# Expert rows stored in slot order and fetched back per token instead of scatter-added; half of the shared tiles moved to the end

## The chip, the cores and the metric

One core of a Trainium2 chip runs the whole program. The metric is the device time of one launch in microseconds (us), lower is better. The engines are named as in the profile: PE (TensorE matmul), PEld (its weight loads), DVE (VectorE), ACT (ScalarE), POOL (GpSimd) and SP (SyncE, which here only issues DMAs). POOL's DMAs go through the software queue q0, those of SP and ACT through hardware queues.

## The reference, cut to what matters

A token embedding, a causal attention of 16 heads, and a mixture of experts over 2048 tokens with 512 channels. The change lies in the last part:

```python
logits = xt @ Wr.T + bias                      # xt: layer-normed rows, 2048 x 512
topk_val, topk_idx = top_k(softmax(logits), 2) # 16 experts
w = topk_val / (sum(topk_val) + EPS)
g, u = einsum('th,ehi->tei', xt, Wg), einsum('th,ehi->tei', xt, Wu)   # i = 256
y = einsum('tei,eih->teh', silu(g) * u, Wd)
routed = einsum('tke,tk,teh->th', one_hot(topk_idx), w, y)
shared = silu(xt @ sWg) * (xt @ sWu) @ sWd
return (routed + shared) + h                   # h: the residual
```

## The kernel before

The tokens are 16 tiles (NT) of 128 rows. After the attention (up to about 640 us) a loop makes the output projection, the second layer norm and the router logits of every tile. `acc[:, c, :]` holds the residual rows of tile c in SBUF; the normed rows go to `xn2_dram`, and turned into `xnT`.

Then come 16 shared tiles (`for n in range(SHARED)` in `moe_pe`, `moe_dve`, `moe_act`): gate and up as split matmuls (three matmuls of 512 columns for each k, L1180), the silu on ACT, the product on DVE (`gate`, L1108), two transposes (L1262), high and low parts (`turn_high` on ACT, `turn_low` on DVE, L1114), the down matmuls (L1273), and `shared_add` (L1119), which adds them to acc. POOL splits the rows of tile c into high and low parts (`split_rows`). SP's `store` writes each finished acc tile to `out`.

Between these tiles DVE and PE make the routing plan. `weights` normalises the two probabilities and makes the one-hots of the choices. `ranks` (PE, after shared tile 3) counts. `places` and `choice_places` give each of the 2 x 2048 choices a slot: slots are grouped by expert and padded to tiles of 128, so there are at most 47 tiles (TILES = 2 * 16 + 15). `slot_onehots` makes three small one-hots for each of 32 pairs of choice and tile, and `slots` (PE, L1243) multiplies them into bank 1: for every slot its token number and its weight. `slot_tokens` turns these into `slot_tok`, `slot_w` and `slot_out` (spare slots get a row behind the output's end). Only then may POOL gather rows.

The 47 expert tiles are loops over pairs of tiles. For tile n PE's `routed` runs two k-steps of gate and up (L1252), the transposes of tile n-1's gated rows, two more k-steps, the transposes of the next tile's gathered rows (`turn_rows`, L1295), and tile n-1's down matmuls (`down_of`, L1331). SP loads expert e+4 into a ring of four (`w_gu`, in the space of `attnT`, and `w_dn`) when expert e's last tile is done, and waits for it to land before it looks at the next one. ACT's `y_scale` (L936) multiplies a tile's result by `slot_w` into one of two `y_sb` buffers. POOL's order is: `gather` of one tile (copy of the row numbers, L829, then an indirect DMA, L832), then `add` of an earlier one (L843, L846), an indirect DMA that adds y_sb to rows of `out` in DRAM. Each add waits for the one before to have landed (`s_yadd`), because two slots can name one token:

```python
pool.wait_ge(s_yc, 2 * m + (s + 1))
if not first:
    pool.wait_ge(s_yadd, 16 * (2 * m + s))
```

The first add also waits until all 16 tiles of acc are stored. The program ends when the last add has landed.

## Time and profile before

| | before |
|---|---|
| median of 3 runs | 1129.62 us (1126.68 to 1134.97) |
| profiled execution, span | 1135.9 us |
| PE busy | 1009.3 us, 89% |
| DVE busy | 560.7 us, 49% |
| ACT busy | 498.4 us, 44% |
| POOL busy | 328.1 us, 29% |
| chain that ended last, largest line | DMA out<-y_sb,out_no 15% |
| DMA, share of 16 engines: hardware queue q1, software queue q0 | 24.9%, 12.1% |

The profile is of one execution; its span is 6.3 us over the median of the other runs. Busy shares are means over stages with different limits: a change is read from the stage it touches. A wait is charged to what released it last. "Issue" is time in which an engine waited for nothing that the profile shows.

### The profile page before, as it was taken

What the parts mean: (1) busy time and instruction counts of PE and PEld (TensorE: products, weight loads), DVE (VectorE), ACT (ScalarE), POOL (GpSimd) and SP (SyncE); (2) the same over time, 40 slices, a digit from 0 to 9 for tenths busy, and PEclk for the clock granted to TensorE, in tenths of its full rate; (3) what the DMA queues carried; (4) which work ended last, traced back from release to release, by engine and by line L of the source; (5) the groups of instructions that cost most, each with busy time, mean ns of one, the idle gap of its engine ahead of it and who ended that gap; (6) DMA issues with size and microseconds to landing.
All of it is one profiled execution on the core that took longest, in us unless ns stands there. A gap on an engine that the chain in (4) does not pass through costs nothing.

```text
span 1135.9 us, 22815 instructions
## 1 busy us (share of the span) xinstructions
PE 1009.3 (89%) x6879; PEld 641.0 (56%) x6880; DVE 560.7 (49%) x1422; ACT 498.4 (44%) x1195; POOL 328.1 (29%) x444
## 2 busy tenths in 40 slices
PE   3766789999989999899998899899898998899994
PEld 1323547677665857567685687778543443344441
DVE  8986336565644756365666677578311111111110
ACT  4802167676756767476768522211121222122221
POOL 4068311110101010010202046333144543444442
PEclk9969989999989999899999999899899999999997
DMA  0023624150523324042335111611396448744442
GB/s 11 29 50 106 171 56 109 38 127 16 117 65 75 76 51 100 31 103 48 76 79 184 57 66 56 260 47 49 97 290 186 78 89 238 231 86 86 81 89 40
DMA packets 40395, 109.11 MB, mean 96 GB/s; under 512 B 9252, under 2 KB 9252, under 8 KB 37986
## 3 DMA queue, kind: packets, MB, share of 16 engines
q1 hardware_dynamic: 27970, 81.89, 24.9%
q0 software_dynamic: 12320, 25.90, 12.1%
q8 instruction: 55, 0.90, 0.3%
q14 instruction: 50, 0.41, 0.1%
HBM read 53.03 MB, written 25.17 MB: 69 GB/s over the span
## 4 chain that ended last, share of the span: by engine, by line
PE 56%; DMA 16%; issue 10%; DVE 9%; POOL 4%; ACT 2%; POOLq 1%; ACTq 0%; DVEq 0%
DMA out<-y_sb,out_no 15%; PE psum L511 10%; PE psum L477 7%; PE psum L524 6%; PE psum L498 6%; PE psum L482 5%; PE psum L1252 4%; PE psum L1196 4%; PE psum L1180 3%; PE psum L1331 2%; PE psum L1273 1%; PE psum L500 1%; PE psum L527 1%; DVE nmax L634 1%; DVE oh_lo L1488 1%
## 5 line engine op out<-in xcount | busy, mean ns | idle before, releaser
L634 DVE TENSOR_REDUCE nmax<-psum 128x1 f32<-128x128 f32 (+7 forms) x256 | 192.2, 753 | 80.2 <-PE psum L500 69.3
L593 ACT ACTIVATE probs<-psum,nmax 128x128 f32<-128x128 f32 (+7 forms) x256 | 190.4, 744 | 52.1 <-DVE nmax L634 46.9
L1252 PE MATMUL psum<-attnT,x_T 128*128 x376 | 183.2, 610 | 10.8 <-issue 9.4
L498 PE MATMUL psum<-k_stack,q_stack 128*128 128x512 f32 (+2 forms) x384 | 157.8, 465 | 24.1 <-issue 15.6
L511 PE MATMUL psum<-ident,probs 128*128 128x128 f32 x1152 | 175.7, 279 | 3.4 <-DVE probsT L580 1.5
L1153 DVE COPY x_T<-psum 128x512 f32<-128x512 f32 x47 | 32.5, 691 | 253.0 <-PE psum L1295 253.0
L578 ACT COPY probsT<-psum 128x512 f32<-128x512 f32 (+3 forms) x256 | 128.9, 503 | 57.0 <-PE psum L511 44.7
L477 PE MATMUL psum<-xnT,w_unit 128*128 128x512 f32 x256 | 132.4, 607 | 0.2 <-ACT full L452 0.2
L511 PEld LDWEIGHTS psum<-ident,probs 128*128 128x128 f32 x1152 | 125.2, 143 | 8.9 <-DVE probsT L580 3.8
L424 POOL CAST part_hi<-full 128x512 fp32r<-128x512 f32 x32 | 19.6, 612 | 378.7 <-ACT full L452 270.8
L1252 PEld LDWEIGHTS psum<-attnT,x_T 128*128 128x128 f32 x376 | 65.8, 193 | 90.0 <-issue 89.7
L498 PEld LDWEIGHTS psum<-k_stack,q_stack 128*128 128x128 f32 x384 | 69.4, 203 | 66.7 <-issue 33.5
L1331 PE MATMUL psum<-w_dn,gated_T 128*128 x188 | 88.6, 594 | 1.0 <-ACT gated_T L905 1.0
L846 POOL DMA_INDIRECT out<-y_sb,out_no x47 | 75.4, 1604 | 44.4 <-POOL out_no L843 44.4
L524 PE MATMUL psum<-probsT,v_unit 128*32 128x128 f32 x2304 | 78.8, 282 | 0.8 <-ACT probsT L578 0.8
L936 ACT ACTIVATE y_sb<-psum,slot_w 128x512 f32<-128x512 f32 x47 | 32.3, 687 | 105.8 <-PE psum L1331 101.9
L524 PEld LDWEIGHTS psum<-probsT,v_unit 128*32 128x32 f32 x2304 | 61.2, 113 | 28.7 <-ACT probsT L578 19.4
L648 DVE TENSOR_TENSOR attnT<-psum,z_rows 128x128 f32 (+1 forms) x64 | 18.6, 291 | 117.3 <-ACT z_rows L600 117.3
L482 PE MATMUL psum<-w_unit,xnT 128*128 128x128 f32 x512 | 66.7, 275 | 0.3 <-DVE full L456 0.3
L580 DVE COPY probsT<-psum 128x128 f32<-128x128 f32 (+3 forms) x128 | 61.6, 481 | 2.7 <-PE psum L511 2.6
L832 POOL DMA_INDIRECT x_rows<-xn_scratch,rows_no x47 | 50.0, 1064 | 42.2 <-POOL rows_no L829 36.1
L482 PEld LDWEIGHTS psum<-w_unit,xnT 128*128 128x128 f32 x512 | 61.8, 192 | 0.5 <-issue 0.5
(223 smaller groups left out, 1507.8 us busy)
## 6 DMA issues: line engine op xcount, KB each, us to landing
attnT<-in_wgu SPq DMA_DIRECT2D x16, 1024.0 KB, 5.1
q_stack<-part_hi SPq DMA_DIRECT2D x64, 128.0 KB, 2.4
q_stack<-part_lo SPq DMA_DIRECT2D x64, 128.0 KB, 2.4
k_stack<-part_hi SPq DMA_DIRECT2D x64, 128.0 KB, 2.4
k_stack<-part_lo SPq DMA_DIRECT2D x64, 128.0 KB, 2.5
w_dn<-in_wd SPq DMA_DIRECT2D x16, 512.0 KB, 6.0
out<-acc SPq DMA_DIRECT2D x17, 256.0 KB, 2.1
h_scratch<-hot_vec SPq DMA_DIRECT2D x16, 256.0 KB
```

The costliest lines, as they stand in the source:

```text
L477: mm = pe.matmul(bank(7), w_unit[:, k, side * P:(side + 1) * P], xnT[:, k, t0:t0 + 512], start=(k == 0), stop=(k == KC - 1), skip_group_ch ...
L482: mm = pe.matmul(bank(7)[:, k * P:(k + 1) * P], xnT[:, c, t0:t0 + P], w_unit[:, c, 2 * P:3 * P], start=(c == 0), stop=(c == KC - 1))
L498: mm = pe.matmul(dst[:, c0:c1], qs, k_stack[b][:, h, c0:c1], start=True, stop=not own)
L511: mm = pe.transpose(bank(4 + m % 2)[:, (j - 4 * k) * P:(j - 4 * k + 1) * P], probs[n % PSLOTS][:, j * P:(j + 1) * P], ident[:, :])
L524: pe.matmul(bank(6)[32 * h:32 * h + 32, 0:P], v_unit[b][:, j, 32 * h:32 * h + 32], probsT[i % 2][:, h, j * P:(j + 1) * P], start=(j == 0), ...
L578: eng.copy(dst, src).then_inc(s_Ca, 1)
L580: eng.tensor_copy(dst, src).then_inc(s_Cd, 1)
L593: act.activation(probs[n % PSLOTS][:, 0:(i + 1) * P], bank(2 * (n % 2), 2)[:, 0:(i + 1) * P], ACT.Exp, bias=nmax[:, n % 4:n % 4 + 1], scal ...
L634: dve.tensor_reduce(nmax[:, n % 4:n % 4 + 1], bank(2 * (n % 2), 2)[:, 0:(i + 1) * P], AX.X, ALU.min).then_inc(s_M, 1)
L846: pool.indirect_dma_start(out=out, out_offset=bass.IndirectOffsetOnAxis(ap=out_no[s][:, :], axis=0), in_=y_sb[:, s, :], in_offset=None, bo ...
L1252: mm = pe.matmul(bank(2 + p), lhs(k), rhs(k), start=(k == 0), stop=(k == KC - 1), skip_group_check=True)
L1331: mm = pe.matmul(bank(6 + p), gated_T[:, p, k * P:(k + 1) * P], w_dn[:, bass.ds(half, 1), k, :].rearrange("p o n -> p (o n)"), start=(k == 0),
```

## The change

Two things are done.

**Scatter to store and fetch.** ACT copies a tile's result unscaled into `y_sb` (`y_copy`) and issues a plain DMA of the 128 rows to a new DRAM tensor `y_dram`, in slot order (`y_store`, two tiles behind). POOL has only gathers in the expert loop. When all 47 stores have landed, POOL fetches for each token tile the two rows of each token (32 indirect DMAs, indices `pos_i`) into a ring of eight tiles, `y_back`, in the space of `attnT`. DVE's `add_choices` adds them, scaled by `w_top`, to acc with two `scalar_tensor_tensor` each. SP stores acc tiles only after that.

**Shared tiles moved.** Only 8 shared tiles (NS) run ahead of the experts, the other 8 behind them. The plan, which was spread over shared tiles 2 to 14, is now made in tiles 2 to 7, with up to 11 one-hot pairs in a tile (it was 5 triples) and a ring of 12. `slot_w`, `slot_pad` and `slot_out` are no longer made, and the weights are computed after the last expert tile. In the tail the splitting of rows (tiles 10 to 15) is on ACT and DVE; POOL splits 8 and 9 early in the expert loop.

The core of the diff:

```diff
-SLOT_RING = 6
-SLOT0 = 6
+SLOT_RING = 12
+SLOT0 = 5
+SLOT_STEP = 11
+NS = 8
+COMB0 = 3
+Y_RING = 8
...
+        def tail_no(c):
+
+            return NS + TILES + (c - NS)
+
+        def pass_of(c):
+
+            return c if c < NS else tail_no(c)
```

SP:

```diff
-            for c in range(NT):
-                store(c)
-
-            sp.dma_start(out[T:T + P, :], acc[:, 0, :]).then_inc(s_pad, 16)
...
-            sp.wait_ge(s_yadd, 16 * TILES)
+            for c in range(NS):
+                sp.wait_ge(s_comb, c + 1)
+                store(c)
```

POOL:

```diff
+            for c in (NS, NS + 1):
+                split_rows(c)
             with pool.Fori(2, TILES // 2) as m:
                 gather(m, 0, False)
-                add(m - 2, 1, False)
                 gather(m, 1, False)
-                add(m - 1, 0, False)
             gather(TILES // 2, 0, False)
-            for j in range(TILES - 4, TILES):
-                add(j // 2, j % 2, False)
+
+            for s in range(2):
+                pool.wait_ge(s_yst[s], 16 * ((TILES + 1 - s) // 2))
+            for c in range(NT):
+                if c >= Y_RING:
+                    pool.wait_ge(s_comb, c - Y_RING + 1)
+                passed(pool)
+                for k in range(TOPK):
+                    pool.indirect_dma_start(
+                        out=y_back[:, c % Y_RING, k, :], out_offset=None, in_=y_dram,
+                        in_offset=bass.IndirectOffsetOnAxis(ap=pos_i[:, k, c:c + 1], axis=0),
+                        bounds_check=TILES * P - 1, oob_is_err=False).then_inc(s_coldg[c % Y_RING], 16)
```

ACT:

```diff
+            def y_copy(n, q, first):
+
+                act.wait_ge(s_y, n + 1)
                 if not first:
...
+                    act.wait_ge(s_yst[q], stored(n, q))
+                act.copy(y_sb[:, q, :], bank(6 + q)).then_inc(s_yc, 1)
...
+            def y_store(j, q):
+
+                act.wait_ge(s_yc, j + 1)
+                rows = slice(j * P, j * P + P) if isinstance(j, int) else bass.ds(j * P, P)
+                act.dma_start(y_dram[rows, :], y_sb[:, q, :]).then_inc(s_yst[q], 16)
...
+            for c in range(NS, NT):
+                n = tail_no(c)
+                if c == NS:
+                    turn_copy(n - 1, 0)
+                else:
+                    turn_high(n - 1)
+                silu(n, n % 2)
+                if c == NS:
+                    y_store(LAST - 1, 1)
+                    y_copy(n - 1, 0, False)
+                    y_store(LAST, 0)
+                if c + 2 < NT:
+                    split_high(c + 2)
+            turn_high(tail_no(NT - 1))
```

DVE:

```diff
+            def add_choices(c):
+
+                r = c % Y_RING
+                dve.wait_ge(s_coldg[r], 16 + 16 * TOPK * (c // Y_RING + 1))
+                step(dve.scalar_tensor_tensor(out=acc[:, c, :], in0=y_back[:, r, 0, :], scalar=w_top[:, c, 0:1],
+                                              in1=acc[:, c, :], op0=ALU.mult, op1=ALU.add))
+                dve.scalar_tensor_tensor(out=acc[:, c, :], in0=y_back[:, r, 1, :], scalar=w_top[:, c, 1:2],
+                                         in1=acc[:, c, :], op0=ALU.mult, op1=ALU.add).then_inc(s_comb, 1)
+                dve.wait_ge(s_comb, c + 1)
...
+            for c in range(NS, NT):
+                if c > NS:
+                    turn_low(c - 1)
+                gate(tail_no(c), tail_no(c) % 2)
+                if c + 2 < NT:
+                    split_low(c + 2)
+                if c > NS + 1:
+                    shared_add(c - 2)
+                if c >= NS + COMB0:
+                    for t in range(2 * (c - NS - COMB0), 2 * (c - NS - COMB0) + 2):
+                        add_choices(t)
+            turn_low(NT - 1)
+            shared_add(NT - 2)
+            shared_add(NT - 1)
+            for t in range(2 * (NT - NS - COMB0), NT):
+                add_choices(t)
```

PE:

```diff
+            for c in range(NS, NT):
+                n = tail_no(c)
+                shared_gate_up(c, 0, 2)
+                turn_gated(n - 1, (n - 1) % 2)
+                shared_gate_up(c, 2, KC)
+                if c == NS:
+                    down_of(n - 1, 0, LAST, expert_half(LAST))
+                else:
+                    shared_down(c - 1)
```

In DVE's shared loop `choices` (the one-hots of the choices, without the weights) runs in tile 2, `places` in 3, `choice_places` in 4, one-hots 0 to 31 in 5, 6 and 7 (11, 11 and 10), `tile_experts` in 6. PE takes one-hots 0 to 10 behind shared tile 6's turn, 11 to 21 behind 7's and the last ten after the loop.

## Rows read from the trace of the kernel before

**Rows 1.** The chain that ended last, 780 to 1136: start, us, what

```profile
1002.55 4.86 DMA out<-y_sb,out_no
...
1008.82 4.69 DMA out<-y_sb,out_no
```

**Rows 2.** The timeline of PE, 800 to 900: start, us, engine, line, operation

```profile
821.62 1.88 PE L1252 MATMUL psum<-attnT,x_T 128*128 x4
...
825.28 0.60 PE L1295 MATMUL psum<-ident,x_rows 128*128 128x128 f32 x4
...
827.43 1.88 PE L1252 MATMUL psum<-attnT,x_T 128*128 x4
```

**Rows 3.** The timeline of PE, around 906, a pair's boundary

```profile
905.37 0.66 PE L1295 MATMUL psum<-ident,x_rows 128*128 128x128 f32 x4
...
908.13 1.98 PE L1252 MATMUL psum<-attnT,x_T 128*128 x4 [0.39 <-issue]
```

**Rows 4.** Busy time by stretch: us, each engine's busy us, granted clock, DMA share, GB/s

```profile
833.58:1111.96 278.38, 255.97 (x756) 114.81 (x757) 42.77 (x84) 60.58 (x126) 128.02 (x167) 1.00 0.59 138
...
724.00:728.00 4.00, 3.48 (x10) 2.76 (x11) 2.81 (x14) 0.58 (x2) 0.10 (x1) 0.57 1.02 423
```

**Rows 5.** The timeline of DVE, 738 to 800: the plan between the shared tiles

```profile
744.68 0.17 DVE L1046 COPY count_e<-psum 128x16 f32<-128x16 f32 x1
...
747.82 0.41 DVE L1114 TENSOR_TENSOR gs_lo<-psum,gs_hi 128x256 fp32r<-128x256 f32 x1
...
748.48 0.68 DVE L1119 TENSOR_TENSOR acc<-acc,psum 128x512 f32<-128x512 f32 x1
749.08 0.41 DVE L1063 TENSOR_TENSOR pos_all<-psum,base_e 128x256 f32<-128x256 f32 x1
...
752.10 0.20 DVE L1071 CAST pos_hlf<-pos_hl 128x64 f32<-128x64 int32 x1
...
754.32 0.83 DVE L1086 TENSOR_SCALAR slot_lo<-iota_f,pos_hlf 128x128 f32<-128x128 f32 x1
...
756.12 0.27 DVE L1086 TENSOR_SCALAR slot_lo<-iota_f,pos_hlf 128x128 f32<-128x128 f32 x1
...
756.74 0.27 DVE L1086 TENSOR_SCALAR slot_lo<-iota_f,pos_hlf 128x128 f32<-128x128 f32 x1
...
794.06 1.54 DVE L1075 TENSOR_TENSOR cmp_j<-tiles_to,iota_j 128x752 f32<-128x752 f32 x1
```

**Rows 6.** The timeline of POOL, 715 to 800 and on

```profile
753.76 1.30 POOL L802 TENSOR_TENSOR xs_lo<-xnT,xs_hi 128x512 fp32r<-128x512 f32 x1
...
800.19 0.18 POOL L829 COPY rows_no<-slot_tok 128x1 int32<-128x1 int32 x1 [5.39 <-DVE slot_out L1102]
```

**Rows 7.** The timeline of PE: shared tiles, then the first expert tile

```profile
740.05 0.48 PE L1180 MATMUL psum<-ws_hi,xs_hi 128*128 128x512 f32 x1
...
744.49 0.39 PE L1180 MATMUL psum<-ws_hi,xs_hi 128*128 128x512 f32 x1
...
805.43 0.63 PE L1295 MATMUL psum<-ident,x_rows 128*128 128x128 f32 x4 [2.17 <-DMA x_rows<-xn_scratch,rows_no]
...
807.22 3.77 PE L1252 MATMUL psum<-attnT,x_T 128*128 x4 [1.16 <-DVE x_T L1153]
```

**Rows 8.** The timeline of POOL, 70 to 140: indirect DMAs back to back

```profile
72.17 1.00 POOL L1413 DMA_INDIRECT hot_vec<-in_hot_emb,hot_row  x1 [0.30 <-issue]
73.47 0.99 POOL L1409 DMA_INDIRECT cold_lat<-in_cold_emb,cold_row  x1 [0.30 <-issue]
```

**Rows 9.** DMA issues of the whole run: count, KB each, median us to landing

```profile
w_dn<-in_wd SPq DMA_DIRECT2D x16, 512.0 KB, 6.0
out<-acc SPq DMA_DIRECT2D x17, 256.0 KB, 2.1
...
x_rows<-xn_scratch,rows_no POOLq DMA_INDIRECT x47, 3.8
```

**Rows 10.** The timeline, 1090 to 1136: the last instruction on POOL

```profile
1126.29 1.57 POOL L846 DMA_INDIRECT out<-y_sb,out_no  x1 [0.93 <-POOL out_no L843]
```

More of the change, by code:

```diff
@@ L284, in build @@
         s_on = sem("out_row_numbers_copied")
-        s_yadd = sem("y_added")
+        s_yst = [sem(f"y_stored{i}") for i in range(2)]
+        s_comb = sem("choices_added")
         s_pad = sem("spare_rows_stored")
@@ L328, in build @@
         s_hotg = [sem(f"hot_gathered{i}") for i in range(NT)]
-        s_coldg = [sem(f"cold_gathered{i}") for i in range(NT)]
+        s_coldg = [sem(f"cold_then_y_gathered{i}") for i in range(NT)]
         s_coldT = sem("cold_turned")
@@ L763, in moe_sp @@
                                          max_val=TILES)
-                    sp.wait_ge(s_y, done + SHARED)
+                    sp.wait_ge(s_y, done + NS)
                     load(WRING * m + s, s)
                     ready(m, s)
-            sp.wait_ge(s_yadd, 16 * TILES)
+            for c in range(NS):
+                sp.wait_ge(s_comb, c + 1)
+                store(c)
+            sp.dma_start(out[T:T + P, :], acc[:, 0, :]).then_inc(s_pad, 16)
+            for c in range(NS, NT):
+                sp.wait_ge(s_comb, c + 1)
+                store(c)
+            sp.wait_ge(s_out, 16 * NT)
+            sp.wait_ge(s_pad, 16)
         def moe_pool(pool):
@@ L815, in moe_pool @@
                     split_rows(c - NT + 3)
-            for c in range(2, NT):
+            for c in range(2, NS):
                 split_rows(c)
@@ L912, in turn_high @@
                 act.copy(gs_hi[:, n % 2, :], bank(4 + n % 2)[:, 0:FF]).then_inc(s_gshi, 1)
-            for n in range(SHARED):
+            for n in range(NS):
                 if n >= 1:
@@ L917, in moe_act, with routed @@
                 silu(n, n % 2)
-            def routed(m, s, first, added):
-                n = SHARED + 2 * m + s
+            def routed(m, s, before, first):
+                n = NS + 2 * m + s
                 q = 1 - s
-                if first:
+                if before < 1:
                     turn_high(n - 1)
@@ L941, in moe_act @@
-            routed(1, 0, False, None)
-            routed(1, 1, False, 16)
-            with act.Fori(2, TILES // 2) as m:
-                routed(m, 0, False, 16 * (2 * m - 2))
-                routed(m, 1, False, 16 * (2 * m - 1))
-            routed(TILES // 2, 0, False, 16 * (LAST - 2))
-            turn_copy(SHARED + LAST, 0)
-            y_scale(SHARED + LAST, 0, 16 * (LAST - 1))
+                if before >= 2:
+                    y_store(2 * m + (s - 2), s)
+                if before >= 1:
+                    y_copy(n - 1, q, first)
@@ L1275, in shared_down @@
                 mm.then_inc(s_y, 1)
-            for n in range(SHARED):
+            for n in range(NS):
                 if n:
@@ L1345, in moe_pe @@
             routed(TILES // 2, 0, True, None)
-            turn_gated(SHARED + LAST, 0)
-            down_of(SHARED + LAST, 0, LAST, expert_half(LAST))
+            for c in range(NS, NT):
+                n = tail_no(c)
[6 more added lines that the diff above has]
+                    shared_down(c - 1)
+            n = tail_no(NT - 1)
+            turn_gated(n, n % 2)
+            shared_down(NT - 1)
         @block.sync
```

145 lines of the change are left out of this document (69 added, 76 removed).

## Prediction

> **What bounds the kernel now.** I read the page's chain first, then the chain of 780 to 1136 alone, then the timelines of PE and POOL in that stretch, and last those of DVE and PE from 725 to 806. Up to shared tile 2 nothing is touched, so only three stretches count: the front (from there to the first expert tile), the expert loop, and what follows the last expert tile.
>
> In the expert loop the chain runs from scatter to scatter: each takes 4.7 to 4.9 us to land, and the next starts 6.27 us after it [rows 1]. The adds wait for each other, and POOL does the gathers between them, so POOL's round of 6.2 us also sets when rows arrive. PE alone would be quicker: an unrolled tile, with its rows there in time, takes 827.43 - 821.62 = 5.81 us [rows 2]. The 42 tiles from the fifth to the last took 278.4 us [rows 4], 6.63 each, or 13.26 a pair. At the boundary of a pair PE shows a gap that no engine is charged with, and the first gate matmul starts 2.76 us after the row transposes [rows 3] where 2.16 would do (the transposes' 0.43 and the down matmuls' 1.72, between the starts in rows 2). I take this as PE's queue, held at the wait for the gathered rows and not able to read ahead over the loop's branch and register loads. If so, the gap comes from a late gather too.
>
> **The front.** Anchors: PE starts shared tile 4 at 740.05 and the next at 744.49, 4.44 us a tile [rows 7], of which gate and up with its transposes are 3.0 and down 1.4 (12 and 6 matmuls of the 18). Without four small weight operations DVE lets PE reach tile 4 about 0.6 us sooner, and `places` now runs at once after `ranks`, at 739.5. From here DVE is the chain. `places` takes 747.82 - 744.68 = 3.14, `choice_places` 752.30 - 749.08 = 3.2; turn_low and gate start 0.33 apart and shared_add takes 0.60 [rows 5]. Added up, one-hot 0 starts at 749.2. A triple takes 756.74 - 756.12 = 0.62, so a pair 0.41 [rows 5]; the first still meets POOL's split, where such an operation took 0.83 and not 0.27 [rows 5, 6], 0.55 more. Eleven pairs end at 754.25. Only then comes turn_low(5), for which PE has waited 2.4 us. PE's down (1.4) frees the ring at 756.4; ten more pairs, 760.6; `tile_experts` 2.65 (1.54 and the two behind it), 763.3; turn_low(6), PE having waited 2.3 us; down, ring free at 765.4; nine pairs, 769.1; PE's last slot matmuls and two operations, 770.1. POOL starts at 770.2 where it started at 800.19 [rows 6], and the first transposes come 5.24 us later [rows 6, 7], at 775.5.
>
> To that I add PE's clock. Rows show it at 0.57 of full, its 1.2 GHz level for most of the stretch, from 724 to 728, behind a wait for the gate [rows 4], and the first expert tile's four matmuls took 3.77 us where four take 1.72 to 1.88, behind waits of 2.17 and 1.16 us [rows 2, 7]. The two new waits of 2.4 and 2.3 us are as long. A down and its slots at the low level cost 1.4 us more, once or twice, some of it under DVE's work: 1.5 in all (bounds 0 and 3.5). The first transposes start at 777.0 instead of 805.4: **28.4 us gained** (22 to 30). The low clock of the first expert tile is in both.
>
> **The expert loop.** The scatters (47 of about 4.8 us) leave; POOL has one gather per tile, about 2.1 us of work and 3.8 to land [rows 9], started when the buffer is free two tiles before it is needed, 11.6 us ahead. Rows are then never late. ACT copies as it did and gets a DMA issue per tile; ACT is 44% busy. A store lands in 2.1 us [rows 9], its buffer is wanted 5.8 us after the issue: covered; a store slower than that would hold y_copy, and down_of behind it. POOL's two `split_rows`, some 4 us, stand once ahead of tile 4's gather and use up a part of its 11.6. SP's weight loads keep their rule: expert e+4 is asked for two tiles ahead of its use, 11.6 us, and both its parts are in 6.5 us later (6.0 for w_dn, issued 0.5 behind [rows 9]) with the scatter beside them; where experts have one tile each, SP's wait for the landing lets the slack shrink by 0.7 a tile, and six such tiles don't end it. I take 11.75 us a pair (11.62 by rows 2, and a little for the branch): 21 pairs 246.8 us, **31.6 us gained**. Bounds: the scatter's pace of rows 1 stays, 12.54 a pair (263.3, gained 15.1); 11.62 (gained 34.4).
>
> **Behind the last expert tile**, counted from its first gate matmul (1111.96 before). PE finishes it in 5.81 less the transposes, 5.4. `weights`, 0.9 us of small operations, runs on an idle DVE behind the last expert tile's gate. Shared tile 8 takes 4.7, with the last expert's down ending at 10.1; y_copy 0.7 (L1119's 0.68 for the same block [rows 5]), issue 0.4, landing 2.1 [rows 9], a start of 0.3, and POOL fetches from 13.6 on. Indirect DMAs stood 1.30 us apart back to back [rows 8]; 32 of them: the last starts at 13.6 + 31 * 1.30 = 53.9 and lands at 57.7. The ring never holds them, for DVE is ahead of it. DVE starts to add in tile 11, when PE has done 5.4 + 4.7 + 2 * 4.44 + 3.0 = 22.1. Its round is then turn_low and gate 0.66, split_low 0.6, shared_add 0.6 and four adds. The trace has no scalar_tensor_tensor of 512 columns from SBUF; the nearest is L1119, 0.68 [rows 5]. With a semaphore between them 0.72 (bounds 0.6 and 1.1): a round is 4.74, more than PE's 4.44, and with the turn through PE and ACT 5.0 to 5.2. So PE is held to DVE's pace. SP's stores of acc, moved from the front to here, go out tile by tile beside the fetches and hold nothing but the last one. The last shared_add ends near 49.2. Six tiles of adds at 1.44 end at 57.8; but the last waits for the fetch, 57.7 + 1.44 = 59.1. Store 2.5, 61.6. From the last landing to the end of the span were 1135.9 - (1126.29 + 4.7) = 4.9 us [rows 1, 10]: 66.5 in all, against 23.9 before: **42.6 us lost** (38 to 55).
>
> **The sum.** 28.4 + 31.6 - 42.6 = 17.4 us gained, 1135.9 to 1118.5 in the profiled execution. That span is 6.3 over the median, so the same difference gives 1129.6 - 17.4 = 1112.2.
>
> **A rule against it.** In the tail POOL makes descriptors for 42 us while DVE reads two SBUF tensors at a time. In the row of 754.32 a DVE operation on SBUF ends at 755.15, just behind POOL's of 753.76 to 755.06 [rows 5, 6]: there one waited for the other to finish. The indirect DMAs of rows 8 kept 1.30 beside DVE work that read mostly PSUM. The Trainium skill's page SBUF — State Buffer (section SBUF: two separate sides) says that the pair of ports which VectorE and GpSimd share is locked for a whole instruction, by a VectorE operation in a two-port mode, or with two SBUF inputs against a GpSimd operation that reads SBUF. The trace agrees with it in that row; whether making descriptors counts as such an operation no row here shows. What it would do is the second rival below, priced from rows.
>
> **The rivals.**
> - The loop keeps its gap: PE's pause at a boundary is the loop's own and no late gather's, 2.76 - 2.16 = 0.60 us a pair [rows 3]. For it: it stands where no engine is named. Against it: the queue had been held at the rows' wait just before. 12.22 a pair, 256.6 us, 9.8 less: 1122; at the bound of 12.54 it is 1129.
> - The other side: in the tail each fetch and each add wait for each other. A fetch then comes every 1.30 + 0.69 = 1.99 us instead of 1.30; 31 * 0.69 = 21.4 more: 1134, slower than before. It decides from 1.30 + 17.4 / 31 = 1.86 us on.
> - The front gives less: DVE's plan loses more to ring waits and to PE's clock (for it: PE then stands over 2 us twice), and the first transposes start at 783, the bound above, 6 us less: 1118.
> - The better case: no clock loss (1.5), 11.62 a pair (2.8), and the tail at its bound of 38 (4.6): 1103.
>
> **How the numbers follow.** Forecast 0.58 (own range 1106 to 1118); better case 0.08; weaker front 0.09; loop with its gap 0.14; the lock 0.09, with the rest 0.02 for the lock together with the bound of 12.54 (1150). The range 1102 to 1128 leaves out the lock and the outer ends. One per cent, about what a measurement can tell from no change, is 1118.3 and 1140.9. Faster: 0.58 nearly whole, 0.08 and part of the front case, 0.67; slower by over 1% where the lock meets another loss, the 0.02 and a third of the 0.09, 0.05; same 0.28.
>
> **What would show it.** First row transposes 27 to 30 us sooner; PE waits for turn_low (L1114's successor) of over 2 us twice in the front; pairs of expert tiles at 11.6 to 11.9 us with no gap at the boundary and no wait for x_rows; 32 fetches 1.30 us apart; DVE adds of 0.7 us; PE's tail tiles near 5 us. Fetches over 1.8 us apart, pairs over 12.3, or a first transpose after 783 would each make it wrong.

## The result

The changed kernel took **1137.45 us** (median of 11 runs, 1135.32 to 1143.70) against 1129.73 us (11 runs, 1126.52 to 1137.31) for the kernel before: ratio **1.0069, 95% interval 1.0049 to 1.0090**. It is slower by 0.7%, which the interval tells from no change though it is less than the 1% that the prediction took for one, and the forecast of 1112 us with its range of 1102 to 1128 is wrong, in its sign too.

The same kernel was then measured five more times, on four chips. On three of them it was faster than the kernel before (0.9913 with 0.9882 to 0.9944; 0.9909 with 0.9879 to 0.9939; 0.9959 with 0.9936 to 0.9983; one single run each at 1128.15 against 1137.65), on the fourth it was slower again, by little (1.0023, 1.0001 to 1.0045). One of six executions of the changed kernel on chip 0 (1209.88 us) and one of 17 of the kernel before (3452.72 us) were slow; the ratios leave them out. The middle of this document is about what divides them.

### The profile of the changed kernel

The profiled execution spans 1139.1 us (the kernel before: 1135.9). First the page's busy times, then PE's timeline where the front ends.

```profile
PE 1008.7 (89%) x6879; PEld 653.7 (57%) x6880; DVE 577.4 (51%) x1424; ACT 497.0 (44%) x1201; POOL 262.9 (23%) x370
```

Columns: start us, us, engine, line, operation, tiles, count, and in brackets the idle time before and what ended it.

```profile
753.71 0.50 PE L1349 MATMUL psum<-ws_hi,gs_hi 128*128 128x512 f32 x1 [1.93 <-DVE gs_lo L1152]
...
777.34 1.09 PE L1372 MATMUL psum<-ident,x_rows 128*128 128x128 f32 x4 [5.68 <-DMA x_rows<-xn_scratch,rows_no]
...
779.43 3.37 PE L1324 MATMUL psum<-attnT,x_T 128*128 x4 [1.00 <-DVE x_T L1200]
```

The first row transposes stand at 777.34, where [rows 7] have 805.43. The loop, from the same view:

```profile
896.39 1.88 PE L1408 MATMUL psum<-w_dn,gated_T 128*128 x4
898.11 1.88 PE L1324 MATMUL psum<-attnT,x_T 128*128 x4
...
901.76 0.60 PE L1372 MATMUL psum<-ident,x_rows 128*128 128x128 f32 x4
902.20 1.88 PE L1408 MATMUL psum<-w_dn,gated_T 128*128 x4
903.92 1.88 PE L1324 MATMUL psum<-attnT,x_T 128*128 x4
...
931.41 2.78 PE L1324 MATMUL psum<-attnT,x_T 128*128 x4 [2.98 <-SPq L754]
...
946.70 1.98 PE L1324 MATMUL psum<-attnT,x_T 128*128 x4 [1.72 <-SPq L754]
```

Tiles start 5.81 us apart (898.11, 903.92), row transposes to next gate 2.16 with no gap: the boundary of [rows 3] is gone, and so is the chain of scatters of [rows 1]: gathers are the only indirect DMAs left in the loop. But PE stands still for weights (L754 is SP's report that they have landed), and the tile after the longer stop runs its matmuls slowly: 2.78 us for four instead of 1.88. From the fifth to the last expert tile the loop takes from 803.83 to 1057.19, 253.4 us against 278.4 in [rows 4].

Behind the last expert tile, first POOL, then ACT with PE's transposes that ACT waits for:

```profile
1071.02 1.00 POOL L875 DMA_INDIRECT attnT<-y_scratch,pos_i  x1 [24.74 <-DMA y_scratch<-y_sb]
1072.32 1.00 POOL L875 DMA_INDIRECT attnT<-y_scratch,pos_i  x1 [0.30 <-issue]
...
1107.67 1.00 POOL L875 DMA_INDIRECT attnT<-y_scratch,pos_i  x1 [0.30 <-issue]
1114.99 1.00 POOL L875 DMA_INDIRECT attnT<-y_scratch,pos_i  x1 [6.32 <-DVE acc L1166]
```

```profile
1087.89 0.38 PE L1334 MATMUL psum<-ident,gated 128*128 128x128 f32 x2
...
1096.25 0.79 PE L1349 MATMUL psum<-ws_hi,gs_hi 128*128 128x512 f32 x1 [6.58 <-issue]
...
1100.72 0.38 PE L1334 MATMUL psum<-ident,gated 128*128 128x128 f32 x2
...
1111.80 0.79 PE L1349 MATMUL psum<-ws_hi,gs_hi 128*128 128x512 f32 x1 [9.31 <-DVE gs_lo L1152]
```

```profile
1077.88 0.37 ACT L923 CAST gs_hi<-psum 128x256 fp32r<-128x256 f32 x1 [2.07 <-PE psum L1334]
...
1095.30 0.37 ACT L923 CAST gs_hi<-psum 128x256 fp32r<-128x256 f32 x1 [7.66 <-remote]
1098.14 0.38 ACT L910 ACTIVATE silu_g<-psum 128x256 f32<-128x256 f32 x1 [2.46 <-remote]
...
1110.85 0.37 ACT L923 CAST gs_hi<-psum 128x256 fp32r<-128x256 f32 x1 [11.82 <-remote]
```

This is where the time went. ACT's copy at 1110.85 needs the transposes that PE's record has at 1100.72 to 1101.10. "remote" is what the view says when a signal came whose sender had been done long before. Matching PE's signals in the trace with the recorded ends of the matmuls that send them gives this (us):

```
sent by              recorded end   arrived   late
shared down L1349       1080.63     1081.71    1.1
transposes L1334        1082.21     1083.85    1.6
gate and up L1253       1083.61     1086.72    3.1
shared down             1086.69     1090.28    3.6
transposes              1088.27     1095.28    7.0
gate and up             1089.67     1098.11    8.4
shared down             1099.18     1103.79    4.6
transposes              1101.10     1110.82    9.7
gate and up             1102.48     1110.90    8.4
```

Everywhere else in this trace PE's signals arrive 0.01 to 0.02 us behind the recorded end (two more, at 78.95 and 79.96, are 0.2 and 0.7 late); those of ACT and POOL are never late. The ends of matmuls are modelled in a profile, so one must ask whether the matmuls themselves were late. The last two lines speak against it: 1.38 us of gate and up matmuls lie between the recorded ends 1101.10 and 1102.48, and the two signals arrive 0.08 us apart (0.07 on chip 14, below). While PE waits, the granted clock falls: its mean over 1088 to 1100 is 0.72, so a part of it ran at the 1.2 GHz level. The tail, from the last expert tile's first gate matmul (1057.19) to the end, is 81.9 us; the forecast had 66.5, the kernel before 23.9.

The ledger: front 28.1 us gained, the four tiles behind it 1.7, loop 25.0, tail 58.0 lost; 3.2 lost in all, 1135.9 to 1139.1.

### The profile page after: what moved, and what is told of

Its sections match the earlier page's. It is cut to its first block, busy times and chain, and to the rows that moved or that the text cites. A ratio compares the mean times of both kernels' runs of the same rounds, so it can differ in the third digit from the quotient of the medians.

```text
span 1139.1 us, 22668 instructions
## 1 busy us (share of the span) xinstructions
PE 1008.7 (89%) x6879; PEld 653.7 (57%) x6880; DVE 577.4 (51%) x1424; ACT 497.0 (44%) x1201; POOL 262.9 (23%) x370
## 4 chain that ended last, share of the span: by engine, by line
PE 61%; issue 14%; DVE 9%; DMA 6%; POOL 3%; another core or an unknown queue 3%; ACT 2%; SPq 1%; ACTq 0%; DVEq 0%; POOLq 0%
PE psum L518 10%; PE psum L484 7%; PE psum L1324 7%; PE psum L531 6%; PE psum L505 6%; DMA w_dn<-in_wd 5%; PE psum L489 5%; PE psum L1269 4%; PE psum L1408 3%; PE psum L1253 3%; PE psum L1349 2%; PE psum L534 1%; PE psum L507 1%; POOL hot_vec L1500 1%
## 5 line engine op out<-in xcount | busy, mean ns | idle before, releaser
L1324 PE MATMUL psum<-attnT,x_T 128*128 x376 | 180.2, 602 | 7.6 <-SPq L754 4.7
L505 PE MATMUL psum<-k_stack,q_stack 128*128 128x512 f32 (+2 forms) x384 | 157.4, 464 | 23.8 <-issue 13.8
L1324 PEld LDWEIGHTS psum<-attnT,x_T 128*128 128x128 f32 x376 | 68.3, 193 | 76.9 <-issue 76.9
L949 ACT COPY y_sb<-psum 128x512 f32<-128x512 f32 x47 | 27.5, 585 | 84.2 <-PE psum L1408 54.6
L910 ACT ACTIVATE silu_g<-psum 128x256 f32<-128x256 f32 x63 | 24.2, 384 | 83.5 <-PE psum L1324 64.1
L507 PE MATMUL psum<-mask_bf,ident_bf 128*128 128x128 bf16 x256 | 59.7, 233 | 0.0
```

Of the source, the lines that this page charges most:

```text
L505: mm = pe.matmul(dst[:, c0:c1], qs, k_stack[b][:, h, c0:c1], start=True, stop=not own)
L507: mm = pe.matmul(dst[:, i * P:(i + 1) * P], ident_bf[:, :], mask_bf[:, :], start=False, stop=True)
L1324: mm = pe.matmul(bank(2 + p), lhs(k), rhs(k), start=(k == 0), stop=(k == KC - 1), skip_group_check=True)
```

## The experiments

Times are compared with the kernel before on the same chip. "Tail" is always from the first gate matmul of the 47th expert tile to the end of the span; line numbers shift by some lines from kernel to kernel.

### The unaltered kernel again: do the late signals belong to it?

> The changed kernel unaltered, looked at once more. In the one trace of it so far, nine of TensorE's signals between 1080 and 1103 us arrive 1.1 to 9.7 us after the recorded ends of their matmuls, and the tail takes 81.9 us from the first matmul of the 47th expert tile. If that belongs to the kernel (theory PAIR: it comes of VectorE's full-width adds together with GpSimd's fetches), the tail is again 75 to 88 us, with three or more such waits of ScalarE of over 2.5 us. If it was an accident of one execution, the tail is 64 to 70 us and the signals are on time.

> The changed kernel unaltered against the kernel before, five rounds. One trace of it has late TensorE signals and a tail of 81.9 us with a time over the kernel before, a second one has none, a tail of 68.4 us and a time 0.8% below the kernel before beside it. Theory CHANCE-OF-THE-EXECUTION (the late signals come and go): times in two groups some 12 us apart, ratio between 0.992 and 1.007. Theory PLACE (the late signals belong to where the first measurement ran, not to each execution): all times of this run in one group, ratio 0.988 to 0.996 if signals are on time here, over 1.003 if they are late.

> The changed kernel unaltered, a third time. If late signals are a matter of where it runs, each place has one kind: either tail 67 to 70 us and a ratio near 0.991, or tail 78 to 86 us and a ratio over 1.00.

> The changed kernel unaltered, a fourth time: either tail 67 to 70 us and a ratio near 0.991 (signals on time), or tail 78 to 86 us and a ratio over 1.00 (late).

> The changed kernel unaltered, a last time: either tail 67 to 70 us and a ratio of 0.988 to 0.998 (signals on time), or tail 78 to 86 us and a ratio over 1.00 (late).

Measured, with the first measurement on top:

```
                chip    changed   before    ratio (95%)               tail   PE signals over 0.3 us late in the tail
first           -       1137.45   1129.73   1.0069 (1.0049-1.0090)    81.9   9, to 9.7 us
after_again     2       1128.15   1137.65   one run each              68.4   none
after_five      0       1129.05   1137.30   0.9913 (0.9882-0.9944)    68.3   none
after_third     10      1126.36   1137.31   0.9909 (0.9879-0.9939)    68.7   none
after_fourth    10      1128.77   1133.35   0.9959 (0.9936-0.9983)    69.0   none
after_fifth     14      1138.66   1135.80   1.0023 (1.0001-1.0045)    81.5   7, to 10.6 us
```

So of the two theories PLACE holds and CHANCE-OF-THE-EXECUTION is out: on chip 14 all ten times of the changed kernel lay between 1135.3 and 1143.6 us, on chip 10 all eleven, of two visits, between 1125.2 and 1131.2; no time jumped from one group to the other. What is not shown is that it is the chip and not the visit, for no place with late signals was measured a second time. The ACT rows on chip 14 are those of the first measurement over again:

```profile
1097.43 0.37 ACT L923 CAST gs_hi<-psum 128x256 fp32r<-128x256 f32 x1 [6.96 <-remote]
1100.99 0.38 ACT L910 ACTIVATE silu_g<-psum 128x256 f32<-128x256 f32 x1 [3.19 <-remote]
...
1113.70 0.37 ACT L923 CAST gs_hi<-psum 128x256 fp32r<-128x256 f32 x1 [11.82 <-remote]
```

and on chip 2 (after_again) the same instructions, with PE named and no long stop:

```profile
1093.79 0.37 ACT L923 CAST gs_hi<-psum 128x256 fp32r<-128x256 f32 x1 [2.72 <-PE psum L1334]
1095.19 0.39 ACT L910 ACTIVATE silu_g<-psum 128x256 f32<-128x256 f32 x1 [1.03 <-PE psum L1253]
1099.20 0.38 ACT L923 CAST gs_hi<-psum 128x256 fp32r<-128x256 f32 x1 [3.62 <-PE psum L1334]
```

What this costs: 81.9 and 81.5 against 68.3 to 69.0, **13 us of the tail**, 1.1% of the time. The ratios lie further apart, 1.6% from 0.991 to 1.007, because the kernel before is not the same everywhere either: its medians go from 1129.73 in the first measurement to 1137.31 on chip 10.

Does it start with the change? No. The trace of the kernel before belongs to the first measurement too (1134.97 us, one of its eleven runs; the chip is not on record), and it has the sign of it, in a stretch that the forecast had used for the pace of indirect DMAs alone ([rows 8], a few us before):

```profile
85.69 0.69 DVE L1548 TENSOR_TENSOR hot_vec<-hot_vec,psum 128x512 f32<-128x512 f32 x1 [2.31 <-remote]
...
87.14 0.58 ACT L1457 COPY xnT<-psum 128x512 f32<-128x512 f32 x1 [1.94 <-remote]
```

There too POOL issues indirect DMAs one after another, and PE's signals arrive up to 3.0 us late (seven of them, with recorded ends between 77 and 87 us, 15.5 us in sum). It costs next to nothing there: the last of the 16 copies to xnT starts at 136.4 us, and at 136.2 in before_ahead on chip 0 (below), which has no late signal. In the same stretch the changed kernel has one signal of PE 0.7 us late where the first measurement ran and one 0.9 late on chip 14. The other 17 traces of this case, on chips 0, 2, 5 and 10, have none over 0.3 us late anywhere. So the mark of the place is there before the changed part of the program begins, though its size differs from trace to trace.

### What in the tail costs what

These kernels were made to find the cause of the late signals, before it was known that they depend on the place. All of them happened to run where signals are on time, so none of them can say what delays signals; they measure the rest of the tail.

**no_fetch**: fetches and adds left out (SP's stores of out then wait for nothing but the end of the expert loop).

```diff
-                    for t in range(2 * (c - NS - COMB0), 2 * (c - NS - COMB0) + 2):
-                        add_choices(t)
...
-                    pool.indirect_dma_start(out=y_back[:, c % Y_RING, k, :], ...)
```

> Left out: the 32 fetches of expert rows and the 32 adds of them (the output has the shared part only). Seen in the changed kernel's trace: in the tail ScalarE waits up to 11.8 us for TensorE's transposes and matmuls that the records have as long done; counted there, TensorE's signals arrive up to 9.7 us after the recorded ends of the matmuls that send them, and only between 1080 and 1111 us, while GpSimd's fetches run. Theory SIGNALS (the fetches that GpSimd issues back to back hold TensorE's signals up): without them the eight shared tiles run at TensorE's own 4.4 us each, no ScalarE wait is over 2.5 us, and the end comes 47 us (44 to 50) after the first matmul of the 47th expert tile instead of 81.9: about 1104 us. Theory ADDS (VectorE's adds and the stores of out do it) says the same for this kernel. Theory CODE (straight-line code of the tail that has to be brought in) keeps waits of 3 to 12 us on ScalarE or TensorE and a time over 1115.

Measured: 1107.72 us (before beside it 1140.95), tail 46.8, no ACT wait over 2.6 us. PE's tail tiles take 4.37 us each and the last down ends 43.6 us after the start. As expected, and it rules out theory CODE where signals are on time; for the late chips it says nothing.

**small_adds** and, on another chip, **small_adds_b**: each pair of adds is one of 128x1.

```diff
-                step(dve.scalar_tensor_tensor(out=acc[:, c, :], in0=y_back[:, r, 0, :], ...
...
-                dve.scalar_tensor_tensor(out=acc[:, c, :], in0=y_back[:, r, 1, :], ...
+                dve.scalar_tensor_tensor(out=acc[:, c, 0:1], in0=y_back[:, r, 1, 0:1], ...
```

> Left out: the adds of the expert rows but for one of one column each (128x1), so that all 32 fetches, their ring of eight and the stores of out stay. SIGNALS: ScalarE's waits for TensorE of 3 to 12 us stay, because the fetches stay as they were; TensorE's last shared tile ends within 4 us of where it did (about 63 us after the first matmul of the 47th expert tile); total 1120 to 1130, since the adds behind the last fetches are gone. ADDS: the waits go, VectorE's rounds shrink to TensorE's 4.4 us, and the end is that of the last fetch, 13.8 + 31 x 1.30 + about 5 = 59 us after the 47th tile's start: about 1116.

> The adds of the expert rows but for one column each are left out. If after_third has its signals on time, this has too, with the tail of 66 us that it had. If after_third has them late: FETCHES ALONE says late here too (tail over 72), PAIR says on time (tail 66).

Measured: 1130.33 (before 1140.95) and 1123.98 us (before 1137.31), tail 66.1 both times, shared tiles done 49.1 and 47.3 us after the start. No signal was late, which at first looked like a proof for ADDS; after_again, unaltered and on time as well, took that away. The end is neither theory's: ADDS wanted a tail of 59, SIGNALS the late waits. What stays: without the adds' 20 us of VectorE work the tail is only 2.3 us shorter (68.4 to 66.1). The fetches set the end, and not by their landing. In small_adds the last add is done 60.4 us after the start and SP has seen all stores landed 62.6 after it; the span ends at 66.1 because POOL's own end comes last. So it is in after_again:

```profile
1115.44 1.27 POOL L875 DMA_INDIRECT attnT<-y_scratch,pos_i  x1 [0.30 <-issue]
```

```profile
L67 POOLq EVENT_SEMAPHORE  x2: 17/17/17, 1125.9 to 1126.0; - x2
L67 POOLq DRAIN  x1: 24833/24833/24833, 1101.0 to 1101.0; - x1
...
L67 SPq DRAIN  x1: 7/7/7, 1125.0 to 1125.0; - x1
```

The first row is from the timeline; the others are from the view of one source line and give durations in ns (shortest, median, longest), then the first and last start. SP is through at 1125.0, but POOL's DRAIN, the last instruction of its queue but for two signals, lasts until 1125.9. In twelve traces of this case the fetches are issued and signals are on time. In eleven of them the span ends 9.37 us after POOL has issued its last fetch, with full adds or small ones (in late_stores, where the stores come last, it is 10.65; in the kernel before 8.07 after the last scatter). What POOL does in that time the trace doesn't say. Where signals are late, the span ends 0.2 us after SP is through: there the last adds and their stores set the end.

**adds_only**: the other half, fetches left out, all adds kept.

```diff
-                dve.wait_ge(s_coldg[r], 16 + 16 * TOPK * (c // Y_RING + 1))
...
-                    pool.indirect_dma_start(out=y_back[:, c % Y_RING, k, :], ...)
```

> Left out: the 32 fetches; the 32 full-width adds stay and read what lies in the buffer (the output is wrong by that), and the stores of out stay. PAIR (fetches and full adds together): signals on time, VectorE's rounds 5.0 to 5.2 us, shared tiles end 47 to 51 us after the 47th tile's start, tail 58 to 63 us. ADDS ALONE (the adds delay TensorE's signals with no fetch beside them): ScalarE waits of 3 to 12 us, tail over 68.

Measured: 1123.17 us (before 1137.65), tail 62.7, shared tiles done at 50.2. Here DVE sets the end, by the last store. So two chains of nearly the same length lie beside each other: fetches alone 66.1, adds alone 62.7, both 68.4.

**plain_rows**: SP fetches 128 neighbouring rows with ordinary DMAs in place of the indirect ones (the sum is then of wrong rows).

```diff
+                for k in range(TOPK):
+                    r0 = (2 * c + k) * P
+                    sp.dma_start(y_back[:, c % Y_RING, k, :], y_dram[r0:r0 + P, :]).then_inc(
+                        s_hl[c % Y_RING], 16)
...
-                    pool.indirect_dma_start(
...
```

> Changed: the 32 fetches are plain DMAs of 128 neighbouring rows each, issued by SyncE in place of GpSimd's indirect ones (the same 256 KB each, other rows, so the sum is of wrong rows). SIGNALS because GpSimd issues them or because they are indirect: no ScalarE wait over 2 us, shared tiles end 45 to 52 us after the 47th expert tile's start, total 1108 to 1118. BYTES (whatever moves 8.4 MB into SBUF at 200 GB/s beside TensorE's tiles holds it up): the waits stay, total over 1125.

Measured: 1119.41 us (before 1140.95), tail 63.1, adds_only's to 0.4 us (a total of 1108 to 1118 was expected): the same 8.4 MB cost nothing when POOL's issuing isn't in it. On this chip, with signals on time, bytes are no bound of the tail.

**paced**: POOL waits until a pair has landed before it issues the next.

```diff
+                if c >= 1:
+                    pool.wait_ge(s_coldg[(c - 1) % Y_RING], 16 + 16 * TOPK * ((c - 1) // Y_RING + 1))
```

> Everything is computed; GpSimd waits for each pair of fetches to land before it issues the next pair. SIGNALS, by the crowd of fetches in flight: ScalarE's waits for TensorE shrink below 2 us, the shared tiles end 45 to 50 us after the 47th expert tile's start instead of 63, but the fetches themselves take 16 x (1.3 + 2.5 to 4) = 61 to 85 us, so the end is 80 to 105 us after it (1137 to 1162). SIGNALS, by the issuing alone (each indirect DMA that GpSimd issues delays TensorE's signals, no matter how many are in flight): waits of half the sum, some 10 to 15 us. ADDS: the adds come at the landings' pace, waits of under 3 us.

Measured: 1183.32 us (before 1140.95), tail 124.3, longer than any case expected. A pair takes 6.6 us, and DVE, which stands at a landing with the next turn_low queued behind it, holds ACT up to 12.4 us and PE with it (shared tiles done at 83.6). PE's signals were on time in it, so ACT's wait is for work and not for a signal. It shows how much it matters that fetches overlap, and that a wait for a landing in DVE's queue is a wait of the shared tiles.

**late_stores**: the stores of out wait for all shared tiles. **late_adds**: the adds come behind all shared tiles.

```diff
+            sp.wait_ge(s_acc, NT)
             for c in range(NS):
```

> Everything is computed; the stores of out begin only when all shared tiles are added. PAIR: the stores have no part in it, so ScalarE's waits of 3 to 12 us stay and the shared tiles end 63 to 72 us after the 47th tile's start. STORES (fetches, adds and SyncE's stores together crowd the DMA engines, and the traffic of stores is what small_adds had too, so this is the weaker one): the waits go, shared tiles end by 52, tail 68 to 74, since 17 stores come at the end.

```diff
                 if c >= NS + COMB0:
-                    for t in range(2 * (c - NS - COMB0), 2 * (c - NS - COMB0) + 2):
-                        add_choices(t)
...
-            for t in range(2 * (NT - NS - COMB0), NT):
+            for t in range(NT):
                 add_choices(t)
```

> Everything is computed; the adds of the expert rows come behind the last shared tile, so that half of the fetches (ring of eight token tiles) run beside the shared tiles with no add beside them. PAIR: signals on time while only fetches run, shared tiles end 43 to 50 us after the 47th tile's start; then 16 token tiles of 1.57 us of adds with 8 more pairs of fetches at 2.6 us: tail 74 to 80 us. FETCHES ALONE: the signals are late from about 24 us after the 47th tile's start as in the changed kernel, shared tiles end at 55 or later, tail over 85.

Measured: late_stores 1129.53 us, tail 69.6, against 68.4 unaltered. So the stores beside the fetches cost nothing; put off, they end last. late_adds 1137.00 us, tail 79.1: the shared tiles end at 43.6, PE's own pace, but POOL then waits 10.8 us for a free slot of the ring. Both beside a before of 1137.65. Where signals are on time it is right to put the adds between the shared tiles, and that is worth 10.7 us.

**all_front**: store and fetch alone, with all 16 shared tiles ahead of the experts (this line, and the parts of the tail that fall away with it).

```diff
-NS = 8
+NS = 16
...
```

> Store and fetch alone: all 16 shared tiles stay ahead of the expert tiles, the 32 fetches and adds follow the last expert tile with no TensorE work beside them. From the changed kernel's rows: first expert tile at 807 us as before, 42 tiles at 5.81 us plus 6 to 9 us for weights instead of 5.88 x 42 plus 30, then 13.8 us from the 47th tile's start to the first fetch, 31 x 1.30 to the last, 4.5 to its landing, 1.6 of adds and 5 us for the last store: tail 65 us. So S = 1087 and the end at 1152, some 14 us (10 to 20) slower than the kernel before. If the forecast's tail model holds (the fetches' issue sets the end), this tail is within 3 us of the changed kernel's where the signals are on time; if VectorE's rounds set it, this tail is 4 to 6 us shorter.

Measured: 1158.27 us, ratio 1.0204 (1.0163 to 1.0246), first transposes at 809.18, tail 65.4, which is 3.0 us less than with shared tiles in it: the edge between the two cases expected. The fetch by itself loses 21 us (10 to 20 were expected), since the 42 us of issuing lie bare; the other half of the change, eight shared tiles laid over it, is worth 29 us (1158.27 to 1129.05 on that chip).

### The loop: why 253 us and not 247

**no_y** (second diff below): no_fetch with the stores of the expert rows left out too. **ahead** (first diff; **ahead_b** on another chip): the whole computation, SP reports an expert ready only after it has issued the next one's load.

```diff
-            for s in range(WRING):
+            for s in range(WRING - 1):
                 ready(0, s)
...
                     load(WRING * m + s, s)
-                    ready(m, s)
+                    if s:
+                        ready(m, s - 1)
+                    else:
+                        ready(m - 1, WRING - 1)
+            ready(E // WRING - 1, WRING - 1)
```

```diff
-                act.dma_start(y_dram[rows, :], y_sb[:, q, :]).then_inc(s_yst[q], 16)
+                act.sem_inc(s_yst[q], 16)
```

**before_ahead**: the first diff's edit in the kernel before.

> Left out: the stores of the expert rows, the fetches and their adds. Theory CONTENTION (256 KB of stores a tile beside the 1.5 MB weight loads make the loads slower): the loads of the stretch with one tile per expert come 0.5 us or more closer than the 8.2 us they have with the stores, and TensorE's waits for weights fall from 7.9 us to under 3. Theory SERIAL (each load starts only after the one before has landed): the pace stays above 7.4 us and half or more of the waits stay.

> Everything is computed; SyncE issues the next expert's weights before it waits for those before them to land (it reports expert e ready after it has issued e+1), so two loads may be under way. In the changed kernel the loads follow one another at 7.2 to 8.6 us where experts have one tile, and TensorE stands still for weights four times, 6.5 to 9.3 us with the slow clock behind it. Theory SERIAL (the pause between one landing and the next load's start makes them late): loads come 1 to 2 us closer, TensorE's waits for weights fall under 3 us and the time falls by 4 to 8 us against the changed kernel, tail unaltered. Theory BANDWIDTH (stores, gathers and weights fill the DMA engines): the pace stays within 0.3 us, gain under 2 us.

> The weight loads issued one ahead, all computed: 0.984 of the kernel before where TensorE's signals are on time, 0.995 to 1.002 where they are late, since it changes nothing in the tail.

> The kernel before with the same edit of the weight loads. There the loop is set by GpSimd's scatter-adds at 11.75 us a pair of tiles and the weights were never late by more than the pace: both theories say no difference, within 2 us of the kernel before.

Measured:

```
               42 tiles us   loads apart us, experts 5 to 10   PE waits for weights us
after_again    253.2         8.5 8.3 8.0 8.5 8.1               6.5
after_five     254.9         8.7 8.1 7.7 8.8 8.6               7.9
after_fourth   252.8         8.4 8.3 8.0 8.0 8.3               6.1
no_fetch       253.3         8.4 8.0 8.5 7.6 7.6               7.9
no_y           249.4         8.0 7.2 7.0 8.4 7.8               4.3
ahead          244.1         5.8 5.8 5.8 5.8 6.1               none
ahead_b        245.4         5.8 5.8 6.1 6.0 6.0               0.9
```

SP's timeline in the changed kernel (first fence) and in ahead (second): the first of each pair of loads.

```profile
801.16 0.34 SPq L748 DMA_DIRECT2D attnT<-in_wgu  x1
...
809.04 0.34 SPq L748 DMA_DIRECT2D attnT<-in_wgu  x1
...
817.21 0.34 SPq L748 DMA_DIRECT2D attnT<-in_wgu  x1
...
825.87 0.34 SPq L748 DMA_DIRECT2D attnT<-in_wgu  x1
```

```profile
801.66 0.34 SPq L748 DMA_DIRECT2D attnT<-in_wgu  x1
...
807.47 0.34 SPq L748 DMA_DIRECT2D attnT<-in_wgu  x1
...
813.27 0.34 SPq L748 DMA_DIRECT2D attnT<-in_wgu  x1
...
819.09 0.34 SPq L748 DMA_DIRECT2D attnT<-in_wgu  x1
```

With two loads under way they go out at the tiles' own pace, though each then takes longer to land (w_dn 9.8 us in the median against 6.8 in after_again; 6.0 in [rows 9]). SERIAL is right and BANDWIDTH is refuted: the DMA engines had room, the pause between one landing and the next load was what made weights late. CONTENTION has a smaller part: without the stores the loads come 7.7 us apart in the mean, 8.0 with them (no_fetch), and 4.3 of 7.9 us of waits stay. The stores' share is about the difference of no_fetch and no_y (two chips), 3.9 us, against the 10.8 and 7.4 that ahead and ahead_b get back with the stores in place (each beside the unaltered kernel on its chip: after_five, after_fourth). In the kernel before the same edit does nothing (before_ahead: 1136.24 us, ratio 0.9993, 0.9968 to 1.0017), as both theories said, because there POOL sets the pace (of 13.26 us a pair; the 11.75 in the expectation is the forecast for the changed kernel).

**ahead beats both kernels**: 1119.20 us, 0.9840 of the kernel before (0.9812 to 0.9868), and 1118.30 us, 0.9851 (0.9814 to 0.9889); 9.9 and 10.5 us less than the changed kernel beside it. I had expected 4 to 8. Both chips have signals on time; on a chip where they are late it wasn't run.

## Why the prediction was wrong, and where it was right

- **Front: right.** First row transposes forecast at 777.0, measured at 777.34 (774 to 779 in the other runs); the wait for turn_low(5) was forecast at 2.4 and is 1.93. The second wait, forecast at 2.3, did not come: at 763.73 DVE waited 1.41 us for gs_hi from ACT before turn_low(6), and PE for nothing. So the number is better than the account of it. The rival "weaker front" (783) is out.
- **The loop's pace: right, its weights: wrong.** 5.81 us a tile, no gap at the boundary, no wait for x_rows: the rival "the loop keeps its gap" is out, the gap went with the late gathers. The step that failed is "both its parts are in 6.5 us later", with "lets the slack shrink by 0.7 a tile, and six such tiles don't end it". 6.5 came from the median landing of [rows 9]; the loads in fact followed each other 7.9 to 8.7 us apart, so the slack shrank by over 2 us a tile and ended. The loop gained 6.6 us less than the 31.6 forecast. The numbers of the kernel before could have shown it: there the loads went out 7.4 to 7.8 us apart, not 6.5, and a pace of 6.6 a tile had hidden that.
- **The tail where signals are on time: right to 2 us, by two errors that cancel.** Forecast 66.5, measured 68.3 to 69.0. First fetch at 13.6, measured 13.8. Last fetch at 53.9, measured 57.7 to 58.3: a fetch takes 1.18 us in the mean when adds run beside it and 1.01 when none does (20 and 12 fetches of after_again), so they come 1.42 apart and not 1.30. It then landed 5.7 us later, not 3.8. The last add ended at 65.1 instead of 59.1. But from there to the end it took 3.3 us, where I had 2.5 for the store and another 4.9 from [rows 1, 10]. That 4.9 was a part of POOL's own end behind its last scatter (8.07 us after its issue); it does not follow the last store but runs beside it, from POOL's last fetch on, and took 9.37 us here. An add is 0.75 us where I took 0.72.
- **The rival of the lock** is true in kind and small in size: 1.57 between fetches while full adds run one after another (row of 1112.29 below), and 1.78 at the most, where it decides only from 1.86 on. The two fetches of over 1.4 us in this trace stand beside split_low and shared_add (L1223, L1158), as do three in small_adds, where no full add runs. The adds themselves were never longer than 0.81. By the rule of the Trainium skill that was weighed there (SBUF — State Buffer, SBUF: two separate sides) whichever starts first has the shared ports for its whole instruction, and the other is blocked. The trace shows much less, a fetch 0.27 us longer beside adds of 0.75 and other fetches beside adds still at 1.00. Whether issuing a fetch is an operation that the rule means stays open; its 21 us did not come. In the tail of after_again:

```profile
1109.34 1.00 POOL L875 DMA_INDIRECT attnT<-y_scratch,pos_i  x1 [0.30 <-issue]
...
1112.29 1.27 POOL L875 DMA_INDIRECT attnT<-y_scratch,pos_i  x1 [0.30 <-issue]
1113.86 1.27 POOL L875 DMA_INDIRECT attnT<-y_scratch,pos_i  x1 [0.30 <-issue]
...
1121.27 0.75 DVE L1164 SCALAR_TENSOR_TENSOR acc<-attnT,w_top,acc 128x512 f32<-128x512 f32 x1 [1.93 <-DMA attnT<-y_scratch,pos_i]
```

- **What was missing: signals that arrive late.** No rival had a wait between PE and ACT in the tail. Where the forecast's sum says "with the turn through PE and ACT 5.0 to 5.2" for a round, two rounds in a row were 11.4 and 15.6 us in the first measurement (gs_hi at 1083.87, 1095.30, 1110.85) and 12.2 and 16.3 on chip 14; none was over 6.1 in the four traces with signals on time. The ring of eight, which by the forecast never holds the fetches, then held POOL for 6.32 us (row of 1114.99). This is the step that failed and alone makes the sign: the tail was 81.9 us where 66.5 was forecast, and 13 us of the 15 are late signals. With late weights (6.6) and the smaller errors of the tail (1.9) the forecast's 17.4 us gained become 8.9 on a chip with signals on time, which is 0.992 and about what was measured there (0.991 to 0.996), and a loss where they are late.
- **The range** took in 1128 us and no such case. The rival that was to end on the other side had the right place (the tail) and a size not far off (21 us against 15.4 measured) with another mechanism. That it came close is luck.

**What stays open.** What holds the signals back is not shown by a run. From the two traces that have it, this much can be read: it begins 9.6 us after the first fetch in both and before the first full-width add (late from a recorded end of 1080.63, first add at 1081.41), it goes on for 7 us after the adds have stopped (1103.4), and it ends at 1110.8, some 3 us after the last fetch before POOL's pause (1107.67); in the kernel before it stands beside back-to-back indirect DMAs of another kind, with no such add. That points to the fetches and speaks against the adds, but it was only argued: no kernel without fetches, without adds or with plain fetches was measured on such a chip, so POOL's issuing and the traffic of the fetches are not told apart either.

## What to carry to other kernels

Before you count on work laid beside a long train of indirect DMAs, look in the trace for waits ended by a sender that had long been done: they mark signals that arrive late, they can come in one place and not in another, and a chain that goes from engine to engine several times a tile pays for each. When a change lets the bound engine run faster, price every periodic transfer by the spacing at which it was issued and not by its landing time; a serial "issue, wait until landed, report" loses the pause between, and issuing one ahead gave back 7 to 11 us here. Ask what ends the program: in these kernels POOL's last indirect DMA is followed by 9.4 us until the span ends, so it pays to issue it early, and an add or a store beside those 9.4 us costs nothing. And two chains laid over each other (fetches alone 66 us, adds alone 63) leave nothing for either to slip.

## What the runs showed of the hardware

- PE's signals can arrive up to 10.6 us after the recorded end of their matmul while POOL issues indirect DMAs every 1.3 us; ACT's and POOL's were never over 0.3 us late in the same traces, and DVE's at most 1.1 us (at 76 us). It came where the first measurement ran and on chip 14, neither measured a second time, and on none of four other chips; in the loop, with one gather every 5.8 us, it came nowhere.
- An indirect DMA of 128 rows of 2 KB takes POOL 1.00 us alone, 1.18 in the mean beside DVE's adds, 1.27 while they run back to back, and 1.4 to 1.5 now and then; plain DMAs of the same bytes from SP cost the tail nothing.
- POOL's queue is through 9.2 us after the issue of its last fetch has ended, and the span ends 9.37 us after it (eleven traces, to 0.01 us); behind the last scatter-add of the kernel before it is 8.07 us.
- Two weight loads under way go out every 5.8 us (1.5 MB each, beside stores and gathers), where one after another takes 8.2, though w_dn then lands after 9.8 us in the median and not 6.8.
